# Expert slots of an attention and mixture-of-experts kernel: six gather and four result buffers, full-row adds ordered by expert, slot loops written out

## The reference

```python
x = x + wkv(w, u, layernorm(x), ctx)
h = layernorm(x)
probs = softmax(h @ gate_w.T)
weights, selected = top_k(probs, 2)
comb = zeros((T, 8)).at[arange(T)[:, None], selected].add(weights)
g, up = einsum('th,eih->tei', h, expert_gate_w), einsum('th,eih->tei', h, expert_up_w)
expert_out = einsum('tei,ehi->teh', silu(g) * up, expert_down_w)
moe_out = einsum('te,teh->th', comb, expert_out)
sh = sigmoid(h @ shared_expert_gate_w.T) * (silu(h @ shared_gate_w.T) * (h @ shared_up_w.T) @ shared_down_w.T)
x = x + moe_out + sh
```

## Time and profile before

| | us |
|---|---|
| median of 3 runs (lowest to highest) | 603.28 (603.09 to 604.98) |
| profiled execution, its own time | 599.83 |
| its span in the profile | 598.0 |
| PE busy | 500.8 (84%) |
| DVE busy | 422.7 (71%) |
| POOL busy | 385.8 (65%) |
| ACT busy | 271.2 (45%) |

### The profile page before, as it was taken

One profiled execution on the slowest core, in us unless ns is written; L12 is line 12 of the kernel. 1 busy time (PEld: TensorE's weight loads), 2 busy tenths in 40 slices (PEclk: granted clock), 3 DMA queues, 4 the chain that ended last, 5 costly groups with the idle time before them and its releaser, 6 DMA issues.

```text
span 598.0 us, 10419 instructions
## 1 busy us (share of the span) xinstructions
PE 500.8 (84%) x2703; PEld 263.8 (44%) x2704; DVE 422.7 (71%) x980; ACT 271.2 (45%) x530; POOL 385.8 (65%) x455
## 2 busy tenths in 40 slices
PE   1024499899999999999999995799999999999971
PEld 1012255445555555555555452355454444444430
DVE  4497988799999999898989563275555555555540
ACT  1749357575665755747644443122232222222220
POOL 4254146757858588585884351348888888888865
PEclk9999799999999999999999998899999999999995
DMA  6941014114314141132110323226666666666654
GB/s 229 417 156 48 0 54 156 57 37 176 72 53 160 37 176 70 55 123 71 54 36 36 124 23 18 74 62 106 103 105 105 105 106 106 102 103 101 104 69 53
DMA packets 31049, 57.44 MB, mean 96 GB/s; under 512 B 6869, under 2 KB 16995, under 8 KB 29475
## 3 DMA queue, kind: packets, MB, share of 16 engines
q0 software_dynamic: 15408, 20.65, 21.8%
q1 hardware_dynamic: 15602, 36.34, 18.5%
HBM read 37.69 MB, written 19.29 MB: 95 GB/s over the span
## 4 chain that ended last, share of the span: by engine, by line
PE 38%; POOL 19%; issue 18%; DVE 12%; DMA 7%; ACT 5%; POOLq 0%; DVEq 0%; ACTq 0%
PE GU L822 22%; PE DN L837 10%; POOL out L526 9%; DMA out<-xb,idsi 5%; POOL wall L410 3%; PE HT L767 2%; PE XT L767 1%; DVE wall L1102 1%; DVE wall L998 1%; DMA out<-xb 1%; DVE wall L991 1%; POOL wall L384 1%; ACT wall L641 1%; DVE wall L988 1%; POOL nrm L376 1%
## 5 line engine op out<-in xcount | busy, mean ns | idle before, releaser
L822 PE MATMUL GU<-wall,xt 128*128 128x512 f16 x768 | 189.7, 388 | 0.1
L837 PE MATMUL DN<-wall,hx 128*128 128x512 f16 (+1 forms) x618 | 152.0, 383 | 8.1 <-DVE xb L1137 3.6
L526 POOL DMA_INDIRECT out<-xb,idsi x78 | 122.2, 1566 | 30.0 <-issue 23.2
L822 PEld LDWEIGHTS GU<-wall,xt 128*128 128x128 f16 x768 | 76.4, 101 | 69.8 <-issue 7.3
L602 ACT ACTIVATE hx<-HT 128x256 f16<-128x256 f32 x103 | 39.0, 378 | 147.2 <-PE HT L767 147.2
L837 PEld LDWEIGHTS DN<-wall,hx 128*128 128x128 f16 x618 | 60.5, 98 | 83.4 <-issue 11.9
L597 ACT ACTIVATE th<-GU,scl 128x256 f32<-128x256 f32 x103 | 48.5, 471 | 84.3 <-PE GU L822 83.4
L1131 DVE TENSOR_TENSOR hx<-HT,hx 128x256 f16<-128x256 f32 x103 | 43.1, 418 | 57.6 <-ACT hx L602 57.0
L822 PE MATMUL GU<-wall,kb 128*128 x240 | 61.5, 380 | 4.3 <-issue 2.3
L822 PE MATMUL GU<-wall,xnb 128*128 x228 | 58.6, 379 | 0.4 <-DVE xnb L1303 0.4
L518 POOL DMA_INDIRECT xb<-xn_rows,idsi x39 | 40.7, 1043 | 27.1 <-issue 9.8
(11 more groups left out here) (158 smaller groups left out, 735.9 us busy)
## 6 DMA issues: line engine op xcount, KB each, us to landing
wall<-wgu SPq DMA_DIRECT2D x12, 1024.0 KB, 5.2
wall<-wd SPq DMA_DIRECT2D x12, 512.0 KB, 6.2
xb<-x SPq DMA_DIRECT2D x16, 256.0 KB, 2.6
cb<-ctx_t SPq DMA_DIRECT2D x16, 256.0 KB, 2.7
xn_rows<-xnb SPq DMA_DIRECT2D x16, 256.0 KB, 2.3
out<-xb SPq DMA_DIRECT2D x16, 256.0 KB, 3.6
out<-xb,idsi POOLq DMA_INDIRECT x78, 3.8
xb<-xn_rows,idsi POOLq DMA_INDIRECT x39, 3.4
```

Of the source, the lines that this page charges most:

```text
L526: pool.indirect_dma_start(out, bass.IndirectOffsetOnAxis(ap=idsi[:, j:j + 1], axis=0), ye[j % 2][:, h * (H // 2):(h + 1) * (H // 2)], None ...
L822: ins = nc.tensor.matmul(GU[par][:], lhs(xp, c), gate_up(base, wp, c), start=m == 0, stop=m == 3 * HC - 1)
L837: ins = nc.tensor.matmul(DN[:], hx[par][:, hp * IE + c * P:hp * IE + (c + 1) * P], down(base, wp, c), start=start and m == 0, stop=stop an ...
```

## The change

The gather buffers go from four to six and the result buffers from two to four (the latter now lie in the memory of the shared expert's weights). On POOL a gather stands ahead of the add of six slots earlier. A result is added by one DMA over full rows. It no longer waits for the slot before but for all adds of the slots of former experts (for a slot of padding: of all slots before); each of the four result buffers has its own semaphore. From slot 4 on, the four counts to wait for are read from a new table `before_i` by four register loads on POOL, each with a wait and a semaphore increment behind it. DVE works out that table in 16 steps (`earlier_adds`) behind the hidden product of the last shared unit. On PE, ACT and DVE all slots are written out with constant numbers; the expert is loaded once a slot on each.

```diff
-GATHERS = 4
+GATHERS = NB
+RESULTS = 4
...
+WAIT_STEPS = 4 + 3 * RESULTS
...
+        before_i = sb("before_i", [P, RESULTS * NSLOT], I32)
...
-        xg = [xb[:, k * XW:(k + 1) * XW] for k in late[0:GATHERS]]
-        ye = [xb[:, k * XW:k * XW + H] for k in late[GATHERS:]]
+        xg = [xb[:, k * XW:(k + 1) * XW] for k in late]
+        ye = [wall[:, SH0 + r * H:SH0 + (r + 1) * H] for r in range(RESULTS)]
         xe = [kb[:, :].bitcast(F16), xnb[:, :].bitcast(F16)]
...
-        added = sems("added_left added_right")
+        added, waits_rdy = sems("added0 added1 added2 added3"), sems("waits_rdy")[0]
...
-            for h in range(2):
-                sp.wait_ge(added[h], 16 * NSLOT)
+            for r in range(RESULTS):
+                sp.wait_ge(added[r], 16 * ((NSLOT + RESULTS - 1 - r) // RESULTS))
...
-            pool.wait_ge(out_st, 16 * (B - 2))
 
             def gather_tile(j):
 
                 r = j % GATHERS
-                if j >= GATHERS:
+                if j < GATHERS:
+                    pool.wait_ge(out_st, 16 * (B - GATHERS + j + 1))
+                else:
                     pool.wait_ge(gather[r], j // GATHERS * 16)
-                wait_from(pool, weighed, j - GATHERS + 1)
+                    pool.wait_ge(weighed, j - GATHERS + 1)
                 pool.indirect_dma_start(xg[r], None, xn_dram, bass.IndirectOffsetOnAxis(ap=idsi[:, j:j + 1], axis=0)
                                         ).then_inc(gather[r], 16)
 
             def add_rows(j):
 
                 pool.wait_ge(dn_free, j + (B + 1))
-                for h in range(2):
-                    wait_from(pool, added[h], j * 16)
-                    pool.indirect_dma_start(out, bass.IndirectOffsetOnAxis(ap=idsi[:, j:j + 1], axis=0),
-                                            ye[j % 2][:, h * (H // 2):(h + 1) * (H // 2)], None,
-                                            element_offset=h * (H // 2), compute_op=ALU.add).then_inc(added[h], 16)
-            for j in range(GATHERS + 1):
+                if j == RESULTS:
+                    pool.wait_ge(waits_rdy, WAIT_STEPS)
+                for r in range(min(j, RESULTS)):
+                    if j < RESULTS:
+                        pool.wait_ge(added[r], 16)
+                    else:
+                        earlier = pool.value_load(before_i[0:1, r * NSLOT + j:r * NSLOT + j + 1],
+                                                  min_val=16, max_val=16 * ((NSLOT + RESULTS - 1) // RESULTS))
+                        pool.wait_ge(added[r], earlier)
+                        plain(pool, earlier)
+                pool.indirect_dma_start(out, bass.IndirectOffsetOnAxis(ap=idsi[:, j:j + 1], axis=0), ye[j % RESULTS],
+                                        None, compute_op=ALU.add).then_inc(added[j % RESULTS], 16)
+            for j in range(GATHERS):
                 gather_tile(j)
-            pool.wait_ge(out_st, 16 * B)
-            for j in range(GATHERS + 1, NSLOT):
+            for j in range(GATHERS, NSLOT):
                 gather_tile(j)
-                add_rows(j - (GATHERS + 1))
-            for j in range(NSLOT - (GATHERS + 1), NSLOT):
+                add_rows(j - GATHERS)
+            for j in range(NSLOT - GATHERS, NSLOT):
                 add_rows(j)
...
-            expert_unit(0, 0)
-            with act.Fori(0, (NSLOT - 3) // 2) as m:
-                expert_unit(m * 2 + 1, 1)
-                expert_unit(m * 2 + 2, 0)
-            expert_unit(NSLOT - 2, 1)
-            expert_unit(NSLOT - 1, 0, ahead=False)
+            for j in range(NSLOT):
+                expert_unit(j, j % 2, ahead=j < NSLOT - 1)
             unit_hi(N_EXP + NSLOT - 1, 0)
...
+            def expert_unit(j, ahead=True):
+                r = j % GATHERS
+                if j == 4:
+                    pe.wait_ge(last_lo, 1)
+                base = base_of[j]
+                before = shared_down(B - 1, SU - 2 + j) if j < 2 else (base_of[j - 2], True, True, j + (B - 2))
                 pe.wait_ge(g_lo, j + 1)
                 unit(N_EXP + j, r % 2, lambda xp, c: xe[r % 2][:, xp * H + c * P:xp * H + (c + 1) * P], base, before,
-                     (lambda: gathered_t(j + 1, (r + 1) % GATHERS)) if ahead else None)
+                     (lambda: next_slot(j + 1)) if ahead else None)
...
-            with pe.Fori(1, (NSLOT - GATHERS) // GATHERS + 1) as m:
-                for r in range(GATHERS):
-                    expert_unit(m * GATHERS + r, r)
-            for j in range(NSLOT // GATHERS * GATHERS, NSLOT):
-                expert_unit(j, j % GATHERS, ahead=j < NSLOT - 1)
+            def next_slot(j):
+                base_of.append(expert_of(j))
+                gathered_t(j, j % GATHERS)
+            next_slot(0)
+            for j in range(NSLOT):
+                expert_unit(j, ahead=j < NSLOT - 1)
...
+            def earlier_adds():
+                TS, wait_step = nc.vector.tensor_scalar, Link(dve, waits_rdy)
+                cmp = r_cmp.rearrange("p (j e) -> p j e", e=E)
+                padded = before_i[:, 0:NSLOT].bitcast(F32)
+                wait_step(TT(padded, cmp[:, :, E - 1], iotaj[:], ALU.mult))
+                wait_step(TT(cmp, cmp, r_end.unsqueeze(1).to_broadcast([P, NSLOT, E]), ALU.mult))
+                wait_step(nc.vector.tensor_reduce(r_eid, cmp, AX.X, ALU.max))
+                wait_step(TT(r_eid, r_eid, padded, ALU.max))
+                for r in range(RESULTS):
+                    of_r = before_i[:, r * NSLOT:(r + 1) * NSLOT]
+                    wait_step(TS(of_r, r_eid, float(RESULTS - 1 - r), None, ALU.add))
+                    wait_step(TS(of_r, of_r, RESULTS.bit_length() - 1, None, ALU.logical_shift_right))
+                    wait_step(TS(of_r, of_r, 16.0, 16.0, ALU.mult, ALU.max))
+                assert wait_step.n == WAIT_STEPS
             shared_tile(B - LAG, last_of_mix)
...
+                if u == 3:
+                    earlier_adds()
...
-            def expert_rows(j, r):
-                e = dve.value_load(span(eidi[0:1, :], j, 1), min_val=0, max_val=E - 1)
-                if isinstance(j, int) and j < 2:
+            expert_at = []
+            def expert_rows(j):
+                if j == 0:
                     dve.wait_ge(out_st, 16 * B)
-                else:
-                    for h in range(2):
-                        dve.wait_ge(added[h], j * 16 - 16)
+                if j >= RESULTS:
+                    dve.wait_ge(added[j % RESULTS], 16 * (j // RESULTS))
                 dve.wait_ge(weighed, j + 1)
                 dve.wait_ge(dn, j + (N_EXP + 1))
-                nc.vector.tensor_scalar(ye[r], DN[:], scale(e, YINV), span(wsl, j, 1), ALU.mult,
+                nc.vector.tensor_scalar(ye[j % RESULTS], DN[:], scale(expert_at[j], YINV), span(wsl, j, 1), ALU.mult,
                                         ALU.mult).then_inc(dn_free, 1)
 
-            def expert_unit(j, q, ahead=True):
-                r = q % 2
-                e = dve.value_load(span(eidi[0:1, :], j, 1), min_val=0, max_val=E - 1)
+            def expert_unit(j, ahead=True):
+                r = j % 2
+                expert_at.append(dve.value_load(span(eidi[0:1, :], j, 1), min_val=0, max_val=E - 1))
                 if ahead:
                     gathered_lo(j + 1, 1 - r)
                 hidden_lo(N_EXP + j - 1, 1 - r)
 
-                nc.vector.tensor_scalar(span(wsl, j, 1), span(xg[q], e + H, 1), 1.0, None,
-                                            ALU.mult).then_inc(weighed, 1)
-                if isinstance(j, int) and j == 1:
+                nc.vector.tensor_scalar(span(wsl, j, 1), span(xg[j % GATHERS], expert_at[j] + H, 1), 1.0, None,
+                                        ALU.mult).then_inc(weighed, 1)
+                if j == 1:
                     accumulate(B - 1)
-                if not (isinstance(j, int) and j < 2):
-                    expert_rows(j - 2, r)
-                hidden(N_EXP + j, r, e)
+                if j >= 2:
+                    expert_rows(j - 2)
+                hidden(N_EXP + j, r, expert_at[j])
...
+            for j in range(NSLOT):
+                expert_unit(j, ahead=j < NSLOT - 1)
                 if 0 < j < 3:
                     last_expert_lo(j - 1)
-            with dve.Fori(1, (NSLOT - GATHERS) // GATHERS + 1) as m:
-                for q in range(GATHERS):
-                    expert_unit(m * GATHERS + q, q)
-            for j in range(NSLOT // GATHERS * GATHERS, NSLOT):
-                expert_unit(j, j % GATHERS, ahead=j < NSLOT - 1)
-            expert_rows(NSLOT - 2, NSLOT % 2)
+            expert_rows(NSLOT - 2)
             hidden_lo(N_EXP + NSLOT - 1, 0)
```

More of the change, by code:

```diff
@@ L202, in build @@
         ids_zero, ids_zst, ids_ld, ids_f, ids_t, ids_rdy = sems("ids_zero ids_zst ids_ld ids_f ids_t ids_rdy")
-        gather = sems("gather0 gather1 gather2 gather3")
+        gather = sems("gather0 gather1 gather2 gather3 gather4 gather5")
```

(51 more changed lines are left out.)

2 lines of the change are left out of this document (removed).

## The result

The changed kernel is slower: 610.09 us median of 4 runs (608.97 to 613.21) against 603.88 before (4 runs too, one more than the 603.28 was taken from), ratio 1.0109 (95% interval 1.0083 to 1.0135). Timed again beside the experiments it gave 1.0114 (1.0089 to 1.0138). The profiled execution took 608.97 us, its span is 607.0 against 598.0.

What follows compares the result with a forecast made beforehand. POOL was taken to bound the kernel. Loop -15.3, front +4.4 and +1.7, tail +3.4 made -5.8 us: span 592.2 instead of 598.0, median 597.5 us instead of 603.3; own range 592 to 601.5, 8 in 10 within 592 to 609.

Steps and rivals of the forecast that it cites:

- What bounds the kernel before: Slot loop: POOL, never resting, was said to bound it at 5.07 us a slot, against PE's own need of 4.54.
- The full-row add costs one issue: POOL's adds: a full row was taken to issue in 1.57 us, like a half, leaving POOL's engine 3.19 us a slot.
- the rival with twice the issue: POOL's adds: full row issues in 3.14 us, engine needs 4.76 a slot, 609 us in all, slower; chance 0.10.
- Slots written out, 4.54 us a step: PE's slot loop: all 34 steps were to take 4.54 us each, 154.4 us instead of 169.7.
- the 15.3 us: Slot loop: gain forecast over 34 steps, from 169.7 to 154.4 us.
- The front, 4.4 + 1.7 us: Ahead of PE's first slot: 4.4 us for DVE's 16 table steps, plus 1.7 lost at half clock after PE's idling.
- Four register loads, costed at nothing in the loop: POOL's sequencer: loads of 0.68 us each, 2.7 a slot, were to hide under DMA issue, round 3.0 us, under 4.54.
- 1.3 us of slack a slot: POOL in the loop: slack per slot to win back some 2.5 us of delay at an expert's first slot.
- 6.1 us had been forecast: Tail: loads ahead of the last three adds, put at 2.7 (four), 2.0 (three) and 1.4 us (two).
- The mechanism was named among the rivals: Rival: POOL's sequencer becomes the bound once a load with what follows passes 1.06 us; 617 us, slower; chance 0.11.
- Landing at 4.1 us: Tail: each full-row add was taken to land 4.1 us from its start (3.7 to 5.3).
- 1.2 us behind the last landing: Kernel's end: the span was to end 1.2 us after the last add lands, at 592.2.

Runs made afterwards that it cites:

- e10: The kernel before with only the slot loops of PE, ACT and DVE written out: 602.97 us, ratio 1.0013 to before.
- e2: The changed kernel with the four register loads per add replaced by waits on constants of this routing: 592.52 us, ratio 0.9863 to before.
- e3: The changed kernel with both edits, table of earlier adds computed early and waits on constants in place of loads: 586.34 us, ratio 0.9764 to before.
- e5: e1 without the load and wait for the result buffer the slot itself reuses, so three loads on POOL: 592.22 us, ratio 0.9864 to before.
- e6: e1 with three loads and waits per add moved from POOL to SP, POOL waiting on one semaphore: 586.86 us, ratio 0.9772 to before.
- e1: The changed kernel with the 16 table steps moved ahead of DVE's wait for the token lists: 600.21 us, ratio 1.0000 to before.
- e11: The changed kernel itself, unaltered, timed again on a chip of the experiments: 609.4 us, ratio 1.0114 to before.
- e7: e3 with only the kernel's very last add made as two half-row adds: 587.95 us, ratio 0.9778 to before.
- e4: The kernel before with one full-row add in place of two half-row adds, still in order by slot: 626.32 us, ratio 1.0436 to before.
- e8: e3 with every add made as two half-row adds, each half with its own four semaphores: 619.59 us, ratio 1.0306 to before.

## Why the prediction was wrong

- **What bounds the kernel before** was right: POOL. e10 brings PE to 4.54 us a step for as long as POOL isn't late, and the time doesn't move.
- **The full-row add costs one issue** was right: 1.58 us, and the rival with twice the issue is out.
- **Slots written out, 4.54 us a step** was right as PE's own pace: 4.53 in e2, e3, e5 and e6. In the changed kernel it was 4.68, and of the 15.3 us only 10.4 came. The ground for it was thinner than said: the earlier trace rows show two written-out steps of 4.54, not three, and a third of 5.08.
- **The front, 4.4 + 1.7 us** was right in mechanism and size: e1 against e11 gives some 7 us, of which up to 1 can be the late start told of below, e3 against e2 6.2.
- **Four register loads, costed at nothing in the loop** is the step that failed. It had two parts. The sequencer's round was put at 3.0 us and is 4.22. The load itself was right (0.29 us, 0.65 with what follows); missing were the fourth load, held for 0.6 us beside the gather's issue, and 0.76 us between the last load and the add, paid in each round and not only in the tail. And the borders were said to be won back with 1.3 us of slack a slot; there were 0.32 us of it, and 1.4 to 4.0 us over the round to win back every four or five slots, behind 5.5 us of lag from the first five adds, which the prediction didn't see at all. e2, with constants, has the slack forecast (a round of 3.19), and there the same lag is won back by slot 13. With the loads POOL fell 6 to 9 us behind and stayed there, gathers came late, and the lag was still 5.7 us when the tail began. With the tail, where 6.1 us had been forecast, the loads cost 14 to 15 us in all (e11 against e2, e1 against e3), 8 to 9 more than the sum had; the account of the trace below finds 6.6 of these, 5.1 up to the last full unit and 1.5 up to add 36. The mechanism was named among the rivals, with a threshold that was wrong: it asked whether the round passes 4.54 us, where it matters as soon as the slack doesn't cover the borders.
- **Landing at 4.1 us** was undersized: 4.85, 4.40 and some 4.5, so 0.5 us for each of three. In the loop the median is 4.8 (e1 to e3). The gathers' 3.4 us was undersized as well: their median in e1 to e7 is 4.2 to 4.3, and one on the chain of waits of after, from 451.42, takes 5.17. What that alone costs was not measured.
- **1.2 us behind the last landing** was taken over from before (598.0 - 596.9 is 1.1) and became 5.2 by the drain: 4.0 us, which nothing in the trace of before hinted at.
- The profiled span of after also runs some 2.8 us later than the one of before from about 348 us on, ahead of the slots: PE makes 13 products at half clock between 348.5 and 352 us, where it makes 21 at full clock before. The traces of e11 and e10 have this too (10 products), those of e1 and e3 don't, and e10 has none of the change but the loops written out. What brings it, and whether it belongs to the change, stays open.

Made up in the trace: 592.2 forecast, 2.8 for that late start, 5.1 to the last full unit, 1.5 to add 36, 1.0 to add 38, 4.4 to the end: 607.0.

The doubt that the Trainium skill's page DMA: Bandwidth & Descriptors raised (section Latency and other measured facts, a floor of about 600 ns for a register load) wasn't borne out as a length, 0.29 us in the median of 140 loads. Its direction was right: loads were what this change paid for, by their place in the round, and those that begin while a gather is issued are above that floor in most cases (0.88 to 0.95 us).

## What to carry to other kernels

Work in a sequencer hides beside its engine only up to the slack of a whole round, and the round includes the dispatch of each DMA; set the slack against waits that come every few rounds, since a lag that isn't won back lasts to the end. Put loads and waits that guard one engine's DMAs on an engine that is idle, and make loads ahead of the wait: each load behind a landing lengthened the way from one add to the next by 0.7 to 1.0 us. Sixteen steps of DVE, 0.2 us each for the most part, cost 6 to 7 us where PE waits for them, and nothing where DVE stands idle anyway, a few instructions earlier.

## What the runs showed of the hardware

- A register load on POOL's sequencer takes 0.29 us in the median while an add is being issued, and 0.88 to 0.95 in most cases if it begins while a gather is. It isn't POOL's own sequencer that makes the difference: in e6 10 of SP's 14 loads that begin within a gather's issue take 0.83 to 0.93 us, against a median of 0.26 outside of one.
- A full-row add of 2 KB a row is issued as fast as one of 1 KB (1.58 us), but lands in 4.8 us in the median in place of 3.8. In the old order, by slot, one full row for each slot costs 5.49 us a step (e4) and two halves 4.99, since a half is issued while the other one is in flight.
- Gathers land in 3.4 to 3.5 us in the median in kernels with half-row adds (before, e8) and in 4.2 to 4.3 in those with full rows (e1 to e7).
- POOL's final drain ends 0.9 to 1.4 us after the last landing in the kernels with 150 indirect DMAs and 4.6 to 5.0 us after it in those with 111 or 112, whatever the last one is; why is open.
